# Splitting the causal mask of a fused attention kernel between TensorE and GpSimd

## The reference

```python
q = apply_rotary(rmsnorm((x @ Wq.T).reshape(B, T, 2 * H, hd)), cos, sin)      # 16 halves of 16
k = apply_rotary(rmsnorm((x @ Wk.T).reshape(B, T, 2 * H, hd)), cos, sin)
v = (x @ Wv.T).reshape(B, T, H, 2 * hd)                                       # 8 heads of 32
scores = jnp.einsum('bhqd,bhkd->bhqk', q, k) * (1.0 / math.sqrt(hd))
scores = jnp.where(causal[None, None], scores, -jnp.inf)
attn = softmax(scores).reshape(B, H, 2, T, T)
attn = attn[:, :, 0] - lam * attn[:, :, 1]
out = layernorm(jnp.einsum('bhqk,bhkd->bhqd', attn, v)) * (1.0 - LAMBDA_INIT)
h = h + out @ Wproj.T
```

## Time and profile before

| what | value |
|---|---|
| median of 3 runs | 630.43 us (628.07 to 630.53) |
| profiled execution, its time | 626.41 us |
| profiled execution, its span | 624.7 us |
| TensorE matmul busy | 523.6 us, 84% |
| VectorE busy | 505.2 us, 81% |
| ScalarE busy | 322.5 us, 52% |
| GpSimd busy | 278.1 us, 45% |
| first and last exponential start | 95.5 us and 358.4 us |

### The profile page before, as it was taken

How to read it: one execution, slowest core, us unless ns; L and a number is a source line. 1 busy time by engine, 2 the same in 40 slices (tenths; PEclk the granted TensorE clock), 3 DMA queues, 4 the chain that set the end, 5 groups by cost and what they waited for, 6 DMA issues and landing times. The chain is left out here.

```text
span 624.7 us, 13838 instructions
## 1 busy us (share of the span) xinstructions
PE 523.6 (84%) x3686; PEld 412.6 (66%) x3686; DVE 505.2 (81%) x1288; ACT 322.5 (52%) x735; POOL 278.1 (45%) x357
## 2 busy tenths in 40 slices
PE   5577678988888888888888747499999999999995
PEld 4465555655665556665566525398888888888885
DVE  4998967888878888888888774688888888888883
ACT  2234236766666666666666732544444444444432
POOL 3354445444444444444544312255555555555541
PEclk9988889999999999999999977799999999999998
DMA  7800001011111111111111111021111111111110
GB/s 205 325 18 16 26 24 36 28 35 43 45 37 45 35 40 45 37 45 37 37 45 38 39 40 31 20 66 51 51 51 51 51 51 51 51 51 51 43 42 28
DMA packets 34154, 32.10 MB, mean 51 GB/s; under 512 B 6130, under 2 KB 32466, under 8 KB 34130
## 3 DMA queue, kind: packets, MB, share of 16 engines
q1 hardware_dynamic: 34130, 31.82, 17.3%
HBM read 23.09 MB, written 8.71 MB: 51 GB/s over the span
## 5 line engine op out<-in xcount | busy, mean ns | idle before, releaser
L904 ACT ACTIVATE pt<-bank 113x452 f32<-113x452 f32 x128 | 59.7, 553 | 32.9 <-PE bank L818 32.9
L1272 POOL TENSOR_TENSOR h_deq<-fh,fhb 128x704 f32<-128x704 f32 x29 | 40.3, 1390 | 78.1 <-DVE fhb L1179 56.3
L152 PE MATMUL bank<-wgu_hi,fx_hi 128*128 128x512 f32 x174 | 70.0, 402 | 5.4 <-DVE fx_lo L1226 5.4
L975 POOL TENSOR_TENSOR rope<-rope,trig 113x256 f32<-113x256 f32 x64 | 62.0, 988 | 20.2 <-DVE rope L1014 20.2
L152 PE MATMUL bank<-wgu_lo,fx_hi 128*128 128x512 f32 x174 | 67.1, 386 | 0.0
L152 PE MATMUL bank<-wgu_hi,fx_lo 128*128 128x512 f32 x174 | 66.9, 384 | 0.0
L1286 POOL TENSOR_TENSOR fh<-fh,fhb 128x704 f32<-128x704 f32 x29 | 40.4, 1395 | 42.1 <-DVE fhb L1240 42.1
L152 PE MATMUL bank<-wqkv_hi,xo_hi 128*113 128x256 f32 (+1 forms) x128 | 48.6, 380 | 11.4 <-DVE rope L1014 11.4
L152 PE MATMUL bank_a<-wd_hi,fh_hi 128*128 128x256 f32 x174 | 55.0, 316 | 2.8 <-DVE fh_lo L1183 2.8
L1339 ACT ACTIVATE bank_b<-fx 128x256 fp32r<-128x256 f32 x29 | 11.2, 388 | 75.6 <-POOL fx L1279 74.5
L152 PE MATMUL bank_a<-wd_hi,fh_lo 128*128 128x256 f32 x174 | 49.5, 284 | 0.0
(11 more groups left out here) (176 smaller groups left out, 1534.5 us busy)
## 6 DMA issues: line engine op xcount, KB each, us to landing
xb<-h_dram SPq DMA_DIRECT2D x29, 129.0 KB, 2.1
rb<-h_dram SPq DMA_DIRECT2D x29, 128.0 KB, 2.1
h_dram<-h SPq DMA_DIRECT2D x32, 112.9 KB
out<-res SPq DMA_DIRECT2D x28, 128.0 KB, 1.7
px<-in_patches SPq DMA_DIRECT2D x9, 384.0 KB, 8.6
hx<-in_txt SPq DMA_DIRECT2D x32, 77.0 KB
hr<-in_txt SPq DMA_DIRECT2D x32, 77.0 KB
wf<-in_wgu SPq DMA_DIRECT2D x1, 1408.0 KB, 7.4
```

The source lines that it names most:

```text
L152: last = pe.matmul(dst, a(k), w(k), start=(start and n == 0), stop=(n == len(passes) - 1))
L904: act.activation(pt[0:T, r, :, :].rearrange("p s t -> p (s t)"), sc_ps[r][0:T, :], ACT.Exp, scale=1.0 / math.sqrt(HD)).then_inc(m["exp_mad ...
L975: pool.tensor_tensor(dst[:, :, half, :], src[:, :, 1 - half, :], table, ALU.mult).then_inc(m["qk_sin"], 1)
L1272: pool.tensor_tensor(blocks(h_deq[:, 0:INTER], BLK), blocks(h_code[:], BLK), spread(h_scale[:], BLK), ALU.mult).then_inc(f["h_deq"], 1)
```

## The change

The mask of banks 0 and 1 stays with TensorE. Banks 2 and 3 get no mask matmul (their score matmuls start the bank afresh); instead GpSimd sets to zero the exponentials of later keys, in place in `pt`, with one `affine_select` for each of the two banks (113 partitions x 452 float32). These stand in GpSimd's list between `sines` and `rope_sum`. ScalarE makes the exponentials in the order 2, 3, 0, 1. `pv` also waits for both selections.

```diff
+        ADDED = NG // 2
...
-                for r in range(NG):
+                for r in range(ADDED):
                     pe.matmul(sc_ps[r][0:T, :], ident_16[0:T, 0:T], mask_16[0:T, :], start=True, stop=True)
...
                         mm = pe.matmul(sc_ps[r][0:T, c * SLOTS * T:(c + 1) * SLOTS * T], k_t[rows, c, :],
                                        q_blk[rows, c, :, :].rearrange("p s t -> p (s t)"),
-                                       start=False, stop=True, skip_group_check=True)
+                                       start=(r >= ADDED), stop=True, skip_group_check=True)
...
             def pv(s, odd):
 
                 pe.wait_ge(m["exp_made"], NG * s + NG)
+                pe.wait_ge(m["masked"], (NG - ADDED) * (s + 1))
                 pe.wait_ge(m["v_staged"], s + 1)
...
-                    (0, exps, 0), (0, exps, 1), (0, exps, 2), (0, exps, 3), (2, squares), (-1, z_square),
+                    (0, exps, 2), (0, exps, 3), (0, exps, 0), (0, exps, 1), (2, squares), (-1, z_square),
...
+            def masks(s, odd):
+
+                for n, r in enumerate(range(ADDED, NG)):
+                    pool.wait_ge(m["exp_made"], NG * s + n + 1)
+                    pass_wait(pool, pool_passed)
+                    pool.affine_select(out=pt[0:T, r, :, :], in_=pt[0:T, r, :, :], compare_op=ALU.is_ge, fill=0.0, base=0,
+                                       pattern=[[0, GS], [1, T]], channel_multiplier=-1).then_inc(m["masked"], 1)
...
-                    (2, epsilons), (-4, join_moments), (1, sines), (1, rope_sum)))
+                    (2, epsilons), (-4, join_moments), (1, sines), (0, masks), (1, rope_sum)))
```

More of the change, by code:

```diff
@@ L216, in early_fusion @@
                  "xo_made xo_high xo_low qk_made v_made qk_squared eps_set qk_sums qk_scaled qk_cos qk_sin qk_roped "
-                 "qkt_made kt_copied q_blocked v_staged scores_made exp_made pv_made ot_copied pv_back "
+                 "qkt_made kt_copied q_blocked v_staged scores_made exp_made masked pv_made ot_copied pv_back "
                  "mix_step z_sums z_squared o_made proj_made h2_added h2_ready ones_set")
```

## The result

| | before | changed |
|---|---|---|
| median | 629.25 us | 649.76 us (647.98 to 650.29) |
| ratio | | 1.0327, 95% interval 1.029 to 1.0364 |
| profiled span | 624.7 us | 646.3 us |

The change makes the kernel 20.5 us slower. Here the kernel before has four executions, where the 630.43 us ahead of the prediction was the median of three. Medians are over all executions; without the one slow execution in each of experiments 1 and 9 they would be 0.3 and 0.1 us lower. These are the page's busy times of the changed kernel: TensorE has 9.7 us less to do, GpSimd 33.7 us more.

What follows compares the result with a forecast made beforehand. The prediction took the circle through VectorE's wait for the `hx` load, not TensorE, as the bound. Step delays summed to 26.4 us, taking the profiled 626.4 to 652.8 us, 656.8 on the median; forecast 655, range 643 to 670.

Steps and rivals of the forecast that it cites:

- TensorE's saving is worth nothing: Two mask matmuls fewer a step on TensorE save 0.4 to 0.46 us, swallowed because TensorE is already early for `qk`.
- `pv` is late because the selections stand behind `sines`: In a looped step, GpSimd reaches the selections only after `sines`, so `pv` on TensorE starts 1.74 us late.
- 0.70 us a looped step: Steps 6 to 27: `scale_qk` comes back 0.70 us later each step, 9.3 us for 8.63, together 15.4 us.
- the two float32 rows: GpSimd selections of 8 and 128 elements, giving 0.57 us for 452; the forecast took 0.62 from the bf16 row.
- Steps 3 to 5, 3.2 us: Early attention steps: transposes about 1.2 us late, DMA queue gives back some 0.15 us; 3 x 1.05 = 3.2 us.
- No stretching of the selections: On GpSimd, where `rope_sum` starts now, a pair of selections keeps its 1.24 us; stretched masks, 681 us, had 7%.
- The condition that the prediction set for stretching: GpSimd's selections would be stretched only beside VectorE instructions that have two SBUF inputs.
- The small term of the loop that others swallow: Existing waits swallow 1.04 us of `pv`'s delay; a pair of 0.54 us or less would mean no change, 630 us, 2%.
- The clock stays up: TensorE's granted clock stays at 1.00 (2.4 GHz) although TensorE idles 1.8 us before `pv`.
- the rival was priced at 3 us: TensorE's granted clock drops from 1.0 to 0.5, adding some 3 us to most steps: 750 us, 3%.
- The rival "faster, 617 us, if the masks came before `pv` is reached": TensorE is the bound; with masks done before `pv`, 0.4 us a step comes back, 13 us in all: 617 us, 4%.
- the circle that I had drawn: Looped step of 8.63 us: `hx` load, `ln_sums`, newton, `scale_qk`, `qk` and `pv`, transposes, `xo_made`, next load.

Runs made afterwards that it cites:

- experiment 1: The changed kernel with both selections ahead of `sines` in GpSimd's list instead of behind; 633.28 us, 1.0081 of the kernel before.
- experiment 9: The changed kernel with `sines` on GpSimd waiting for `cosines` on VectorE; 667.57 us, 1.0659 of the kernel before.
- experiment 3: The changed kernel without selections or the wait for them, banks 2 and 3 left unmasked; 629.01 us, 1.0012 of the kernel before.
- experiment 5: The changed kernel with all four mask matmuls kept, so banks 2 and 3 are masked twice; 650.2 us, 1.0337 of the kernel before.
- experiment 2: The changed kernel with both selections moved behind `rope_sum` in GpSimd's list; 703.86 us, 1.1198 of the kernel before.
- experiment 6: The kernel before the change, with only `sines` on GpSimd made to wait for `cosines` on VectorE; 617.1 us, 0.9799 of the kernel before.
- experiment 7: The changed kernel with one bank for GpSimd instead of two, its selection ahead of `sines`; 618.52 us, 0.9839 of the kernel before.
- experiment 4: The changed kernel with one bank for GpSimd instead of two; 633.85 us, 1.0089 of the kernel before.
- experiment 10: The kernel of experiment 7 with the `hx` load ahead of the residual's load in the DMA queue; 616.82 us, 0.9818 of the kernel before.

## Why the prediction was right, and where it was off

- *TensorE's saving is worth nothing*: shown by experiments 3 and 5, from both sides; its wait for `scale_qk` grows by what is saved and goes when the matmuls come back.
- *`pv` is late because the selections stand behind `sines`*: shown. Ahead of them some 16 us come back (1), behind `rope_sum` 54 us more go (2). The amount of GpSimd work is the same in all three.
- *0.70 us a looped step*: it is 0.53 (11.6 us for 22), and this term makes 3.8 of the 5.6 us by which the 31 intervals were over-forecast. The mechanism held; the size of the selection and the gaps around it were off. `pv` is 3.21 us behind `scale_qk` and not 3.44: a selection takes 0.591 us and not 0.62, in all 64 of them between 585 and 596 ns, and there is no gap ahead of the pair. `sines` ends at 254.03 and the pair starts at 253.99 and takes 1.13 us for my 1.24 and 0.07. The lower price, by the two float32 rows, was 0.57, and the measured one lies between it and the bf16 row. The rest of the sum went as told: transposes 0.90 us behind `pv`, load 0.23 us behind `xo_made`, where I allowed up to 0.22.

```profile
L958 POOL TENSOR_SCALAR_AFFINE_SELECT pt<-pt x64: 585/591/596, 98.8 to 380.5; 113x452 f32<-113x452 f32 x64
```

- *Steps 3 to 5, 3.2 us*: it is 1.3 us. One interval of the kernel before was 9.36 us, and the changed kernel has 8.90 us there. In the timeline of the kernel before, VectorE waits at that place twice as long as elsewhere for the load:

```profile
134.24 0.43 DVE L1090 BATCH_NORM_STATS2 st_in<-hx 113x6 f32<-113x256 f32 x1 [1.98 <-DMA hx<-in_txt]
```

  It is one slow transfer: the second part of that load was issued at 130.88 and VectorE starts 3.36 us later, where this takes 1.80 to 2.07 us in the ten other steps read up to 195 us. Without it the kernel before would have taken about 1.4 us less in steps 3 to 5 (experiment 3, which has no such transfer, takes 24.25 us there), and the delay would be 2.7 us, near the forecast. Experiment 6 has such a transfer at the same place (an interval of 9.35 us), experiment 5 has two at others, experiment 7 has none (7.88). What slows it stays open; that it fell on the kernel before and not on the changed one was chance for this comparison.
- *The small term of the loop that others swallow*: experiment 4 shows the threshold. One selection moves `pv` by 1.0 us and a looped step by 0.07.
- *No stretching of the selections*: right, 585 to 596 ns, beside VectorE instructions that take one operand from PSUM. The condition that the prediction set for stretching is met in experiments 1, 7 and 10, where a selection runs beside `cosines`: there the longest takes 1.11, 1.04 and 1.01 us.
- *The clock stays up*: right at waits of 1.41 to 1.49 us (1.00 from 130 to 360 us). Experiments 2 and 9 have it falling at longer waits, though not at all of them, and at no more than 1.2 us a step in experiment 2, where the rival was priced at 3 us.
- *The rival "faster, 617 us, if the masks came before `pv` is reached"*: wrong as a price. Experiment 1 meets its condition nearly (a wait of 0.2 us) and gives 633 us, since another circle through `rope_sum` and the roots stands just behind. I had reasoned with one path at a time; moving a piece in one engine's list moves all pieces behind it.
- What I had before me and did not use: `cosines` at 0.69 or 1.22 us and `sines` at 0.72 or up to 1.24. I asked only whether the masks would be stretched. The overlap of those two was worth 11 us and lay in the circle that I had drawn.

On the whole the median came at 649.8 us for 655 forecast, inside the range of 643 to 670 and on the side that the forecast named; 655 had been taken 1.8 us below the 656.8 of the sum. Part of the nearness is luck. The sum put the profiled execution at 652.8 us, and it came at 648.0, while errors of both signs stood in it: the 0.9 us of step -1 that nobody forecast, and the slow transfer. The step from the profiled execution to the median, taken as 4.0 us, was 1.8 us.

## What to carry to other kernels

When work moves to an idle engine, ask first where in that engine's list it stands and what its consumer waits for; 3% were lost here by work that fits easily into the idle time of GpSimd. Price the saving by what ends the giving engine's next wait: here TensorE waited for something else right behind the saved work, by only a third of a microsecond a step, and the saving was worth nothing. And compare the quickest and the usual duration of each instruction on the circle: where they differ by nearly two, something runs beside it, and starting that something later can be worth more than the change at hand.

## What the runs showed of the hardware that I had not expected

- GpSimd and VectorE slow each other when both read two SBUF operands. `cosines` (113x512) takes 0.69 us alone and 1.22 us beside `sines`; two `sines` instructions (113x256) take 1.42 us alone and 1.89 to 1.97 us beside it. In such a pair one takes 0.75 to 0.84 us and the other 1.17 us; the median of 1.00 us in the earlier trace rows lies between the two groups and is the duration of neither. This is what the Trainium skill says ("GPSIMD Engine Reference", Key points: GpSimd shares its SBUF interfaces with VectorE and contends with instructions of two SBUF inputs), and the trace agrees; that section gives no size, and here both lose, VectorE 77% and GpSimd a third or more. One step of the kernel before:

```profile
L975 POOL TENSOR_TENSOR rope<-rope,trig x2: 751/962/1174, 248.3 to 249.0; 113x256 f32<-113x256 f32 x2
```

- With one operand GpSimd can lose alone. The selections ran in 585 to 596 ns beside VectorE instructions that take one operand from PSUM. In experiment 1 `cosines` starts first and keeps its 0.68 us, while the selection that starts behind it takes 0.85 to 0.90 us for 0.59; in experiment 7 likewise, 0.67 to 0.80 us in the steps from 200 to 251 us. In step 0 of experiment 1 the selection starts 0.10 us ahead, and there `cosines` takes 1.03 us and the selection 1.04 us: both lose. Durations of `cosines` and `sines` over the whole span with `sines` behind `cosines` (experiment 6):

```profile
L1020 DVE TENSOR_TENSOR rope<-rope,trig x32: 682/684/694, 88.2 to 340.4; 113x512 f32<-113x512 f32 x32
...
L975 POOL TENSOR_TENSOR rope<-rope,trig x64: 718/728/743, 89.0 to 341.9; 113x256 f32<-113x256 f32 x64
```

- On GpSimd a selection starts some 0.04 us before the instruction ahead of it, on which it does not depend, ends in the records (253.99 and 254.03 in the changed kernel), even with a wait and a semaphore increment between them; I had allowed 0.07 us for a gap.
- TensorE's granted clock stayed at 2.4 GHz in all 25 steps of the changed kernel between 130 and 360 us, with waits before `pv` of 1.41 to 1.49 us. It fell to 1.2 GHz for some microseconds in 20 of 24 steps with 1.98 to 2.90 us (experiment 2) and in 8 of 23 with 1.27 to 1.90 us (experiment 9); in these 8 the wait was 1.70 us or more, but the same waits stood in steps without a fall. What else decides it is not shown.
